# Three layers of a transformer block on one core: the routed experts' first norms computed in the last steps of the first attention, and a new order in the first steps of the block attention

## The reference, cut to what matters

```
x = x + tanh(g_xattn[0]) * attention(layernorm(x), ctx)           # 16 heads of width 8, over features
x = x + tanh(g_ffn[0])   * experts(layernorm(x))                  # 64 experts, top 8, and a shared one
x = x + tanh(g_xattn[1]) * mlstm(layernorm(x), ctx)               # 16 heads of width 16, gated cells
y = layernorm(x); a = y + attention(layernorm1(y))                # 16 heads of width 128, causal
x = x + tanh(g_ffn[1])   * (a + moe(layernorm2(a)))               # 4 experts, top 2
```

## Time and profile before

| what | value |
| --- | --- |
| time, median of 3 runs | 1650.48 us (1650.08 to 1655.21) |
| the profiled execution | 1649.62 us, its span 1648.2 us |
| busy PE / DVE / ACT / POOL | 95% / 67% / 60% / 40% of the span |
| mean granted clock of PE | 0.978 of full speed |
| experts begin / mLSTM begins / block attention begins | about 305 / 899 / 1013 us |

### The profile page before, as it was taken

The page is one execution under the profiler, slowest core; times in us unless marked ns, Lnnn a source line. Parts: engine busy times, 40 slices in busy tenths (PEclk is TensorE's granted clock), DMA queues, the critical chain, the costliest instruction groups (busy, mean ns, idle before and its releaser), DMA issues.

```text
span 1648.2 us, 30409 instructions
## 1 busy us (share of the span) xinstructions
PE 1567.2 (95%) x10956; PEld 1255.7 (76%) x10956; DVE 1098.9 (67%) x2085; ACT 987.6 (60%) x2013; POOL 660.1 (40%) x582
## 2 busy tenths in 40 slices
PE   5699999689999999999999998999999999999999
PEld 3256555378888888888887455778888888889888
DVE  5788886479644446444445667888868877787665
ACT  4388888544433334433333666767787787787553
POOL 3333333123435333333333034767455457555100
PEclk8699999899999999999999999999999999999999
DMA  7656664353343433333330003344334443542320
GB/s 218 187 168 199 202 203 152 110 144 94 99 128 108 116 100 113 106 109 108 106 105 11 8 5 125 116 130 140 122 120 137 137 145 123 180 148 84 78 52 26
DMA packets 111047, 196.24 MB, mean 119 GB/s; under 512 B 16721, under 2 KB 59541, under 8 KB 108073
## 3 DMA queue, kind: packets, MB, share of 16 engines
q1 hardware_dynamic: 110802, 194.27, 39.1%
q10 hardware_dynamic: 96, 0.01, 0.0%
HBM read 167.64 MB, written 25.73 MB: 117 GB/s over the span
## 4 chain that ended last, share of the span: by engine, by line
PE 49%; issue 22%; POOL 13%; DVE 8%; ACT 4%; DMA 3%; SPq 1%; POOLq 0%; DVEq 0%; ACTq 0%
POOL e_hidden L1080 12%; PE bank L68 8%; PE bank L70 8%; PE bank L69 8%; PE bank L283 4%; PE bank L321 3%; PE bank L2100 3%; PE bank L2132 3%; PE bank L307 3%; PE bank L2122 1%; PE bank L1385 1%; PE bank L1384 1%; PE bank L1395 1%; ACT b_turned L2206 1%; DVE b_straight L2296 1%
## 5 line engine op out<-in xcount | busy, mean ns | idle before, releaser
L1080 POOL TENSOR_TENSOR e_hidden<-e_gated,e_comb_wide 128x512 f32<-128x512 f32 x132 | 211.1, 1599 | 342.4 <-DVE e_gated L1045 326.8
L917 ACT CAST e_hidden_hi<-e_hidden 128x512 fp32r<-128x512 f32 x132 | 82.0, 621 | 316.6 <-POOL e_hidden L1080 316.6
L1036 DVE TENSOR_TENSOR e_hidden_lo<-e_hidden,e_hidden_hi 128x512 fp32r<-128x512 f32 x132 | 98.1, 743 | 209.8 <-ACT e_hidden_hi L917 209.8
L70 PE MATMUL bank<-e_x_hi,e_weights_lo 128*128 128x512 f32 x520 | 206.2, 397 | 0.0
L68 PE MATMUL bank<-e_x_hi,e_weights_hi 128*128 128x512 f32 x520 | 205.2, 395 | 0.7 <-ACT e_comb_rows L877 0.7
L69 PE MATMUL bank<-e_x_lo,e_weights_hi 128*128 128x512 f32 x520 | 205.2, 395 | 0.0
L2206 ACT ACTIVATE b_turned<-bank,b_swap_bias 64x512 f32<-64x512 f32 x256 | 174.9, 683 | 33.2 <-PE bank L70 28.8
L528 DVE TENSOR_REDUCE a_negmax<-bank 128x2 f32<-128x512 f32 x256 | 164.8, 683 | 35.1 <-PE bank L283 34.4
L2346 POOL TENSOR_TENSOR b_turned<-b_turned,b_rope_q 128x512 f32<-128x512 f32 x64 | 83.0, 1297 | 182.0 <-ACT b_turned L2206 182.0
L424 ACT ACTIVATE a_exp<-bank 128x512 f32<-128x512 f32 x256 | 143.6, 596 | 19.9 <-PE bank L307 11.3
L68 PE MATMUL bank<-e_weights_hi,e_hidden_hi 128*128 128x256 f32 (+1 forms) x528 | 147.7, 280 | 1.7 <-DVE e_hidden_lo L1036 1.7
(11 more groups left out here) (337 smaller groups left out, 4076.1 us busy)
## 6 DMA issues: line engine op xcount, KB each, us to landing
e_comb_wide<-e_combT SPq DMA_DIRECT2D x130, 256.0 KB, 4.0
e_raw<-in_e_weights SPq DMA_DIRECT2D x64, 384.0 KB, 4.5
b_qk_hi<-b_qk_parts SPq DMA_DIRECT2D x64, 256.0 KB, 2.7
b_qk_lo<-b_qk_parts SPq DMA_DIRECT2D x64, 256.0 KB, 3.0
a_qs<-a_q_parts SPq DMA_DIRECT2D x48, 192.0 KB
a_ks<-a_k_parts SPq DMA_DIRECT2D x48, 192.0 KB
b_qk_parts<-columns SPq DMA_DIRECT2D x32, 256.0 KB, 4.1
b_vw_hi<-b_v_parts SPq DMA_DIRECT2D x16, 512.0 KB, 4.2
```

The costliest lines, as they stand in the source:

```text
L70: return pe.matmul(out, w_lo, x_hi, start=False, stop=stop, skip_group_check=True)
L1036: dve.tensor_tensor(lo[rows, :], m.hidden[at % 2][rows, :], hi[rows, :].bitcast(F32), ALU.subtract).then_inc(s.hidden_lo)
L1080: pool.tensor_tensor(m.hidden[i][rows, :], m.gated[i][rows, :], m.comb_wide[u % E_RING][rows, chunk * BANK:(chunk + 1) * BANK], ALU.mult). ...
```

## The change

Two things are changed. (1) In the first attention, the last steps get `norm_early`: for blocks 0 to 7 (the first two chunks, which are complete long before) DVE makes statistics, an inverse root by a guess and three Newton rounds, and the normalised rows, in steps 128 to 135. Pieces 0 to 2 fall away for chunks 0 and 1, with ACT's square root, and PE transposes from the attention's own tile `a_normed`, whose place in memory moves. `split_weights(0)` moves back: on ACT behind piece 4, on DVE behind piece 6. (2) In the seam to the block attention, `b_y` moves from the mLSTM's step 14 to the block attention's step 0; the first fetches of weights are in a new order; groups 2 and 3 of the mLSTM's results are spread anew over the steps; and in the first 12 steps POOL's part of them waits until `rotated` of the step is done.

```diff
+A_HALF = NB // 2
+HALF_STATS, HALF_GUESS, HALF_NEAR, HALF_ROWS = (0, 1), 2, (3, 4, 5), (6, 7)
...
 def layer0_dve(k, m, s, ring):
+    def norm_early(at):
+        for chunk in range(NCHUNK // 2):
+            if at == HALF_STATS[chunk]:
+                dve.wait_ge(s.added, A_HALF)
+                for b in range(CHUNK):
+                    dve.bn_stats(m.stats[chunk][:, b, :], k.resid[:, chunk * CHUNK + b, :]).then_inc(own.tick())
+        if at == HALF_GUESS:
...
+        if at in HALF_NEAR:
+            dve.wait_ge(s.early_near, HALF_NEAR.index(at) + 1)
+            dve.tensor_tensor(step, root, root, ALU.mult).then_inc(own.tick())
...
+        for chunk in range(NCHUNK // 2):
+            if at == HALF_ROWS[chunk]:
...
+                last.then_inc(s.early_normed)
     for t in range(A_STEPS):
...
+        if t >= A_LAST:
+            norm_early(t - A_LAST)
...
 def experts_pe(...):
         if piece == 3:
-            pe.wait_ge(s.normed, chunk + 1)
-            turn(t.norm.rows, 0, bank).then_inc(s.turned)
+            if chunk >= HALF:
+                pe.wait_ge(s.normed, chunk - HALF + 1)
+            else:
+                pe.wait_ge(before.early_normed, chunk + 1)
+            turn(rows, 0, bank).then_inc(s.turned)
...
 def experts_act(...):
     act.wait_ge(before.added, NB)
+    for stored in columns_stored:
+        act.wait_ge(stored, 2 * DMA * (2 * RH // KEPT_SLOTS))
     for piece in range(ROUTE_PIECES):
...
-        if piece == 0:
+        if piece == 4:
             split_weights(0)
...
 def experts_dve(...):
-        if piece == 0:
+        if piece == 0 and chunk >= HALF:
             norm_start(t.norm, src, s.var)
...
-        if piece == 0:
+        if piece == 6:
             split_weights(0)
...
+LAST_SQUARED, LAST_SUMMED, LAST_GUESSED = (0, 2), (1, 3), (2, 4)
+LAST_WEIGHED, LAST_NEAR, LAST_ROOTS, LAST_SCALED, LAST_ADDED = (1, 9), (3, 7), (4, 8), (5, 10), (6, 11)
...
 def attention_sp(k, m, w, s, ring, before):
-    sp.wait_ge(before.cells, NB)
+    sp.wait_ge(before.arguments, SLOTS * NB)
     fetch(w.split_qk, k.qk_parts, 1, ring["qk_in"])
-    for n in range(2):
-        fetch(w.split_o, k.o_parts, n, ring["o_in"])
-    fetch(w.split_v, k.v_parts, 1, ring["v_in"])
     for n in range(B_STEPS + 5):
...
             fetch(w.split_qk, k.qk_parts, n + 1, ring["qk_in"])
+        if n == 1:
+            sp.wait_ge(before.cells, NB)
+            for i in range(2):
+                fetch(w.split_o, k.o_parts, i, ring["o_in"])
+            fetch(w.split_v, k.v_parts, 1, ring["v_in"])
...
 def attention_dve(...):
+        if n == 0:
+            input_chunk(0, 3)
...
 def attention_pool(...):
+        if n <= LAST_ADDED[-1]:
+            pool.wait_ge(s.rotated, 2 * (n + 1))
         last_cells_pool(k, cells, before, n)
```

More of the change, by code:

```diff
@@ L767, in route @@
         t = m.routers[chunk % HALF]
+        rows = t.norm.rows if chunk >= HALF else early_rows[:, chunk * CHUNK:(chunk + 1) * CHUNK, :]
         if piece == 3:
-            pe.wait_ge(s.normed, chunk + 1)
-            turn(t.norm.rows, 0, bank).then_inc(s.turned)
+            if chunk >= HALF:
[3 more added lines that the diff above has]
+            turn(rows, 0, bank).then_inc(s.turned)
         if piece == 4:
-            turn(t.norm.rows, 1, bank).then_inc(s.turned)
+            turn(rows, 1, bank).then_inc(s.turned)
         if piece == 5:
@@ L858, in route @@
         t, cols = m.routers[chunk % HALF], slice(chunk * BANK, (chunk + 1) * BANK)
-        if piece == 1:
-            act.wait_ge(s.var, chunk + 1)
+        if piece == 1 and chunk >= HALF:
+            act.wait_ge(s.var, chunk - HALF + 1)
             act.activation(t.norm.rstd[:, :], t.norm.rstd[:, :], ACT.Sqrt).then_inc(s.root)
@@ L952, in route @@
         routed, probs, left, best, comb = t.logits[:, :, 0:EXPERTS], t.probs, t.left, t.best, t.comb
-        if piece == 0:
+        if piece == 0 and chunk >= HALF:
             norm_start(t.norm, src, s.var)
-        if piece == 2:
-            dve.wait_ge(s.root, chunk + 1)
-            if chunk >= HALF:
-                dve.wait_ge(s.turned, NCHUNK)
+        if piece == 2 and chunk >= HALF:
+            dve.wait_ge(s.root, chunk - HALF + 1)
             norm_end(t.norm, src).then_inc(s.normed)
@@ L1081, in experts_pool, with layer0_experts @@
                            ALU.mult).then_inc(s.weighed)
-def layer0_experts(k, before, finished):
+def layer0_experts(k, attended, finished):
+    before, early_rows, columns_stored = attended
     with ExitStack() as stack:
@@ L1542, in cells_dve @@
             block.rows()
-        if n == FIRST_Y:
-            block.scaled()
+        if n == FIRST_TABLE:
+            block.table()
     block.low_part()
```

90 lines of the change are left out of this document (52 added, 38 removed).

## The result

The changed kernel takes 1642.59 us (median of 11 runs, 1639.05 to 1648.13) beside 1652.30 us for the kernel before (11 runs, 1648.72 to 1655.21): ratio of the two 0.9949, 95% interval 0.9938 to 0.9961, so 8.4 us less (6.4 to 10.2). The sign and the range held, the latter near its slow end; of the 13.2 us forecast some two thirds came.

The account below looks back on a forecast made before the run. PE bounds nearly everywhere, dipping at seams; DVE bounds block attention steps 6 to 9. Part 1's 7.1 plus part 2's 6.1 makes 13.2 us off 1649.62, so 1636.4; with the median 0.86 higher, 1637, range 1630 to 1644.

Parts of the forecast that it names:

- PE's start: Experts' seam: first transposes wait only for the last addition, 305.45 for 313.61, a shift of 8.2 us.
- What is put on the path: Experts' softmax: e_weights_lo now stands inside it and costs 0.2 to 2.3 us; 1.7 taken.
- From there PE hardly stops; that last time is what counts: Experts' seam: PE hardly stops after the first expert product at 335.58, so that product's start is what counts.
- the 7.1 forecast: Part 1, experts' seam: expert loop starts at about 328.5, a gain of 7.1 us (least 1, most 9).
- It rose again some 5 us after PE took up work: Experts' seam, argument against the context-sums rival: PE's clock rose some 5 us after it took up work at 313.61.
- the context sums hold PE up: Rival, experts' seam: all sums at half clock, loop starts at 334.5, part 1 gives 1.1, time 1643; chance 0.13.
- Part 2, `b_y`: Moved from the mLSTM to block attention step 0: shift of 1.4 us, costing 1.2 in its new place.
- the fetch order's 1.5: Block attention, before step 2: weights land earlier, PE's 2.78 stop goes, 1.5 us comes through.
- the spread: Block attention: group 3's sum and guess leave steps 7 and 8 for 3 and 4, where 0.7 us is lost.
- about 2.0: Block attention: net gain in us by the start of step 6, from 1.4 + 1.5 - 1.2 - 0.7 + 0.6 with some slack.
- Steps 6 to 9: 4.1: Block attention, DVE-bound steps: 4.1 us gained of PE's 4.65 idle; PE idle under 1.5 us expected.
- The "slower" rival: Block attention: POOL's wait for rotated puts up to 2.39 us ahead of sine products in ten steps; 1660, chance 0.05.

Follow-up runs that it names:

- changed again: The changed kernel itself measured once more, as partner of the combined run: 1642.68 us (6 runs), ratio 0.9942 to the kernel before.
- e1: Part 1 alone on the kernel before (early norms, block attention as before): 1646.85 us (12 runs), ratio 0.9968.
- e10: Changed kernel with group 3's guess moved from step 4 to step 9, and its Newton rounds and weights with it: steps 0 to 13 took 99.66 us for 98.97.
- e4: Changed kernel with context_T fetched earlier and b_y back in the mLSTM's step 14: first e_hidden at 29.61 us, steps 0 to 13 98.15 us.
- e3: Changed kernel with DVE's e_weights_lo behind piece 5 instead of 6: comb weights ready at 18.92 us, first e_hidden at 32.12 us.
- e5: Changed kernel with context_T earlier, e_weights_lo behind piece 5 and the old first fetches at the block attention: first e_hidden 29.45, steps 0 to 13 99.01 us.
- e7: Changed kernel with context_T earlier, e_weights_lo behind piece 5, groups 2 and 3 in their old steps: first e_hidden 29.34, steps 0 to 13 101.44 us.
- e8: Changed kernel with context_T earlier, e_weights_lo behind piece 5, 36 PE identity turns before the sums, b_y in step 3: first e_hidden 32.00, steps 0 to 13 98.38 us.
- e9: As e8, plus 16 identity turns ahead of the third chunk's first turn and group 2's weights in step 2: to thirteenth e_hidden 53.58, steps 0 to 13 98.83 us.
- both kernels with the filler: e9 and e11, with 16 PE identity turns ahead of the third chunk's first turn in the experts' loop: 53.58 and 53.54 us to the thirteenth e_hidden.
- e11: Changed kernel with context_T earlier, split behind piece 5, busy tail, 20 turns before the sums, 16 in the loop, b_y in step 3: 1639.39 us, ratio 0.9929.

## Why the prediction was right or wrong

**Part 1, PE's start and the seam: right.** The first turns came 0.06 us after the addition, the norms were done 12.6 us ahead of the last addition's start (`a_normed` ends at 298.54), and the tail kept its length (27.19 us from DVE's last pair of maxima to the last addition, 27.18 before). The loop was forecast at 23.7 from the last addition's start (328.5 - 304.83); measured 24.23, 24.24, 22.82 and 23.72 in the four profiles that have part 1 as it is (changed, changed again, e1, e10). The sums were forecast to end at 22.0; 21.06 to 21.97. "What is put on the path": `e_weights_lo` took 3.09 where POOL had begun first (e1, e4, e10), the upper bound. In the two profiles of the changed kernel it began first, took 0.95, POOL's second `e_x_lo` took 2.97 for 2.34, and DVE's next multiplication then took 1.92 for 0.42. By the Trainium skill ("SBUF — State Buffer", § Who interferes with whom) the one of such a pair that starts first keeps the other out for a whole instruction, and both cases agree with that. The price was 1.3 to 1.5 us for 1.7 where the router products ran at full clock (comb weights at 20.24 in e1 and e4, at 18.7 to 18.9 behind piece 5 in e3 and e5 to e7) and 0.6 where they ran at half (22.80 for 22.18 in e8 and e9). In the first case the sums came later still. In the two profiles of the changed kernel the softmax ended the path, 1.2 and 1.4 us behind the sums, so there part of the 0.6 was paid.

**Part 1, the failed step: "From there PE hardly stops; that last time is what counts".** What counts is the first `e_hidden`, which hangs on the transfers of the comb weights, and the twelve behind it. PE's better clock at the loop's start (before, PE was at 1.2 GHz there) won nothing, and PE came to stops of 1.3 and 2.55 us for one of 1.97. Behind the latter the clock fell in eight of the ten profiles that have the early norms and no filler there, and 1.6 us were lost (55.2 for 53.6); in e3 and e10 it stayed up behind the same stop. In both kernels with the filler the loss is gone. To the thirteenth `e_hidden` the seam took 91.02 and 92.96 us in the two profiles without part 1, and 86.45, 86.07, 84.86 and 84.56 in the four with it as it is: 6.5 us on average for the 7.1 forecast.

**The clock.** "It rose again some 5 us after PE took up work" did not hold: in both profiles of the changed kernel PE worked at half clock through all of the turns and router products, and the comb weights came 2.6 us later than in e1 (22.8 for 20.24). In e1, e3 to e7 and e11 the clock had not fallen yet at the turns. The rival "the context sums hold PE up" got 0.13. In the two profiles of the changed kernel it is not what happened: there the softmax came last, as forecast (comb weights at 22.8 for 22.2). In the ten other profiles with early norms the sums end the path, though with part of them at half clock (8.35 to 9.8 us for 7.07) or late, never with all. The rival's price was too high besides: its 334.5 put 2.9 us between the end of the sums and the first expert product, and 1.75 were measured in e1 and e3.

**Part 2, `b_y`: right.** 1.33 for 1.4 in the mLSTM, and 0.82 for the 1.2 that it was to cost. Its four operations took 2.35 us in step 0.

**Part 2, the failed step: the fetch order's 1.5 as a term of its own.** With `b_y` in step 0 and the clock up the old order gave the same time. The stop on PE and `b_y`'s delay on DVE lie beside each other ahead of ACT's step 2, and only the later one counts; I had added them with opposite signs, +1.5 and -1.2. Together, from step 0 to step 2, they gave 1.7 for that 0.3 (13.66 to 11.95).

**Part 2, the spread: the late steps right in kind, the early ones wrong.** The "about 2.0" forecast by the start of step 6 was 0.0 (1.33 won, 1.33 lost between steps 0 and 6): the guess of group 3 met the sine products, which the prediction had not priced and which cost 2.3 in step 5, and step 2 lost 0.7 (a small `m_total` addition on DVE took 2.20 us for 0.28 beside POOL's weights of group 2). "Steps 6 to 9: 4.1" was 5.9 (32.63 for 38.57), more than the 4.65 that were called all that could be gained, and steps 10 and 11 took back 1.3. PE's idle time in steps 6 to 9 fell from 4.65 to 1.93, not under 1.5. Part 2 as a whole gave 1.33 + 3.35 = 4.7 for 6.1. That this is near is partly luck: 1.4 more than forecast came in steps 0 and 1 and 1.8 more in steps 6 to 9, and some 3 less in steps 2 to 5 and 1.3 less from step 10 on. The "slower" rival is out: POOL's waits won 0.5.

**The sum.** The marks give 6.5 + 4.7 = 11.2 us, the times 8.4 (6.4 to 10.2) and, in the second measurement, 9.6 (7.3 to 11.7). The 6.5 is an average with e1 and e10; the changed kernel's own two profiles give 5.7. And the marks end at step 63: behind DVE's last addition the span goes on for 2.25 us in both profiles without part 1, for 2.9 in both of the changed kernel, and for 2.75 to 3.2 in the ten others with early norms, for a cause that is open. 5.7 + 4.7 - 0.65 = 9.8 lies within both intervals. In the attention between first and last addition the profiles lie anywhere from 197.6 to 200.6 with part 1 and the tail as it is, and at 198.8 and 198.1 without: too few to say whether some more is lost there. That stays open.

## What to carry to other kernels

When a seam gets shorter, look for the transfer and the clock behind it before adding up the gain: here a load issued at the seam's start, which had been hidden, became what PE waits for, and PE then computed at half clock. Of two delays on two engines ahead of the same instruction only the later one counts; put them under a maximum, not into a sum. A stretch in which two engines have no slack (step 9 of the changed kernel: PE idle for 0.00 us, DVE for 0.04) can't take work from a neighbour for nothing, even if that work is a few operations of 0.2 to 0.5 us.

## What the runs showed that I had not expected

PE's granted clock does not follow its work in a way that the marks fix: with the same instructions, the router products ran wholly at 1.2 GHz (7.09 us) in the changed kernel's two profiles and in e8 and e9, and wholly at 2.4 GHz (3.79 us) in the eight others with early norms. Between kernels that are the same there, the comb weights came 2.6 us later where the router products ran at half clock (22.80 in the changed kernel for 20.24 in e1), although `e_weights_lo` was then not held.

DVE operations with one tensor as input are held too: two TENSOR_SCALARs of 128x64 took 1.19 and 1.20 us for 0.20 beside POOL's sine products, and the four of `b_y` 2.35 for 1.37 (the last of them 1.38 for 0.40).
